# A transformer block with modulation on one core: four piece sums of the second modulation, moved from VectorE to TensorE

## What is computed

```
mod = silu(c) @ wmod                      # six rows of 1024
ga, gb = sign * max(|.|, 0.25)            # the two gates
h = layernorm(x) * (1 + ca) + sa
x = x + ga * (h @ masked(weight).T + bias)        # 1024 -> 1024
h = layernorm(x) * (1 + cb) + sb
x = x + gb * (silu(h @ gate_w.T) * (h @ up_w.T)) @ down_w.T    # 1024 -> 2752 -> 1024, int8-range weights
```

## Time and profile before

| | us |
|---|---|
| median of 3 runs | 1171.25 (1168.79 to 1171.27) |
| the profiled execution | 1171.43 |
| its span, first to last instruction | 1169.6 |
| TensorE busy | 1122.1 |
| VectorE busy | 652.5 |
| ScalarE busy | 398.3 |
| GpSimd busy | 340.8 |

### The profile page before, as it was taken

One profiled execution on the slowest core, in us unless ns is written; L12 is line 12 of the kernel. 1 busy time (PEld: TensorE's weight loads), 2 busy tenths in 40 slices (PEclk: granted clock), 3 DMA queues, 4 the chain that ended last, 5 costly groups with the idle time before them and its releaser, 6 DMA issues.

```text
span 1169.6 us, 13023 instructions
## 1 busy us (share of the span) xinstructions
PE 1122.1 (96%) x4773; PEld 529.4 (45%) x4773; DVE 652.5 (56%) x833; ACT 398.3 (34%) x718; POOL 340.8 (29%) x348
## 2 busy tenths in 40 slices
PE   5799999999988989999999999999999999999998
PEld 2544544545443434444444444444444444444444
DVE  3989957866655677767666666654442222222222
ACT  0322036655454434544544554443330000000000
POOL 1133327447634253434354344431110000000000
PEclk9799899999999999999999999999999999999999
DMA  9993221435344345755565555421644433434320
GB/s 345 401 343 79 73 71 37 108 97 164 135 157 122 99 124 168 186 138 148 131 151 139 147 151 142 107 67 42 255 147 169 151 120 139 149 115 149 106 103 36
DMA packets 88736, 167.10 MB, mean 143 GB/s; under 512 B 18592, under 2 KB 53152, under 8 KB 85984
## 3 DMA queue, kind: packets, MB, share of 16 engines
q1 hardware_dynamic: 77168, 125.88, 34.5%
q0 software_dynamic: 11504, 40.38, 11.5%
HBM read 117.47 MB, written 48.76 MB: 142 GB/s over the span
## 4 chain that ended last, share of the span: by engine, by line
PE 77%; DVE 10%; DMA 4%; issue 3%; POOL 2%; SPq 2%; ACT 1%; DVEq 1%; POOLq 0%; ACTq 0%
PE pA L1082 26%; PE pA L1178 12%; PE pB L1082 12%; PE pB L1178 12%; PE pA L962 11%; DVE work L1295 3%; DMA work<-in_L_wmod 2%; PE pB L951 2%; DMA work<-in_L_ffn_up_w 1%; DVE work L1456 1%; DVE work L1309 1%; SPq L451 1%; DVE work L1293 1%; DVE work L1393 1%; DVE small L1196 1%
## 5 line engine op out<-in xcount | busy, mean ns | idle before, releaser
L1082 PE MATMUL pA<-work 128*128 128x512 f16 x1680 | 380.7, 381 | 12.4 <-ACT work L863 6.3
L1082 PEld LDWEIGHTS pA<-work 128*128 128x128 f16 x1680 | 164.6, 98 | 214.8 <-issue 9.3
L962 PE MATMUL pA<-work 128*128 128x512 f32 x512 | 227.2, 599 | 3.1 <-ACT work L770 2.0
L1082 PE MATMUL pB<-work 128*128 128x512 f16 x752 | 176.2, 379 | 1.7 <-DVE work L1456 1.7
L962 PEld LDWEIGHTS pA<-work 128*128 128x128 f32 x512 | 96.3, 192 | 117.0 <-issue 112.3
L692 POOL DMA_DIRECT2D h_scratch<-work x84 | 64.3, 766 | 287.0 <-DVE work L1470 286.8
L1178 PE MATMUL pA<-work 128*128 128x512 f16 x672 | 147.7, 379 | 0.0
L863 ACT ACTIVATE work<-pA 128x512 f32<-128x512 f32 x126 | 75.1, 596 | 195.2 <-PE pA L1082 195.0
L1178 PE MATMUL pB<-work 128*128 128x512 f16 x630 | 138.4, 379 | 0.0
L1470 DVE SCALAR_TENSOR_TENSOR work<-work 128x512 f16<-128x512 f16 x84 | 69.5, 828 | 107.0 <-ACT work L869 107.0
L746 ACT ACTIVATE work<-pB,small 128x128 f32<-128x128 f32 x256 | 92.6, 477 | 87.4 <-PE pB L951 80.9
(11 more groups left out here) (130 smaller groups left out, 972.2 us busy)
## 6 DMA issues: line engine op xcount, KB each, us to landing
work<-h_scratch SPq DMA_DIRECT2D x16, 1376.0 KB, 6.1
h_scratch<-work POOLq DMA_DIRECT2D x84, 256.0 KB, 3.3
work<-in_L_wmod SPq DMA_DIRECT2D x10, 2048.0 KB, 17.7
work<-in_L_ffn_gate_w SPq DMA_DIRECT2D x84, 128.0 KB, 3.7
work<-in_L_ffn_up_w SPq DMA_DIRECT2D x84, 128.0 KB, 3.7
work<-in_L_ffn_down_w SPq DMA_DIRECT2D x96, 112.0 KB, 2.6
work<-in_L_attn_data SPq DMA_DIRECT2D x16, 512.0 KB, 4.4
x_scratch<-work POOLq DMA_DIRECT2D x16, 512.0 KB, 5.6
```

The costliest lines, as they stand in the source:

```text
L962: last = pe.matmul(pA[:, 2 * par(t) + h, :], hT1[par(t)][:, c, :], wT[:, c, h * H:(h + 1) * H], start=(c == 0), stop=(c == KT - 1))
L1082: last = pe.matmul(ps, w[:, m, c], bc[b][:, mv_, s, c], start=begin, stop=(i == n - 1 and c == KT // 2 - 1 and s == 1), skip_group_check=True)
```

## The change

The four pieces 6 to 9 (v = 3 and 4) are summed by `row_sum` on TensorE. The list `ROWS` numbers the row sums: 0 and 1 are the pieces 0 and 2 as before, 2 to 5 are the pieces 6 to 9. The four new sums alternate between the two banks `pB[2]` and `pB[3]`. In tile 2 TensorE makes two of them after `transpose(0, 3)`, ahead of `attend(2, 1)`, and two behind it; ahead of the first stands the wait for `ga_ready`, which was in tile 3. ScalarE copies each row, in two instructions of 256 columns, behind `turn_out(3)`; sums 4 and 5 wait until the bank is copied, and `transpose(1, 0)` in tile 3 waits until all are. `columns(3)` and `columns(4)` wait for the copies and take 1/128 as their right operand. VectorE's four `sum_half` are gone. SP waits in tile 8 for the row sums.

```
@@ -225,7 +225,7 @@
         boundT, boundp = pA[:, 3, P:2 * P], pA[:, 3, 3 * P:3 * P + 4]
         sump = [pB[:, 3, 4 * NB * g:4 * NB * (g + 1)] for g in range(2)]
 
-        rowsum = [pA[:, 0, :], pA[:, 2, :]]
+        rowsum = [pA[:, 0, :], pA[:, 2, :]] + [pB[:, 2 + k % 2, :] for k in range(4)]
         turned = [pA[:, 1, :], pA[:, 3, :], pA[:, 0, :], pA[:, 2, :]]
 
         def turned_at(u):
@@ -325,7 +325,8 @@
 
 
 
-        SUMMED = [1, 3, 4, 5, 6, 7, 8, 9]
+        SUMMED = [1, 3, 4, 5]
+        ROWS = [0, 2, 6, 7, 8, 9]
 
         TURNS = [0, 2, 1, 3, 4, 6, 5, 7]
 
@@ -404,9 +405,7 @@
             return tb_late if r in (2, 3) else tb
 
         def wait_summed(eng, m):
-
-            n = SUMMED.index(m) + 1
-            eng.wait_ge(dve_summed, n + sum(1 for k in SUMMED[:n] if 6 <= k < 10))
+            eng.wait_ge(dve_summed, SUMMED.index(m) + 1)
 
         def mask_rows(eng, r):
             w = wst[r].rearrange("p (b i) -> p b i", i=Q)
@@ -497,7 +496,7 @@
                     sp.wait_ge(xg_ready, t + 2)
                     load_x(t + 3)
                 if t == 8:
-                    wait_summed(sp, 8)
+                    sp.wait_ge(row_summed, 6)
                 if 8 <= t < 8 + EARLY:
                     load_unit(t - 8)
 
@@ -733,9 +732,23 @@
             act.wait_ge(c_loaded, 16)
             act.activation(csil, cvec, ACT.Silu).then_inc(silu_c_done, 1)
 
-            for v in range(2):
-                act.wait_ge(row_summed, v + 1)
-                act.activation(acc[v][:, 0:H], rowsum[v], ACT.Copy).then_inc(row_copied, 1)
+            def copy_row(k):
+                v, h = ROWS[k] // 2, ROWS[k] % 2
+                act.wait_ge(row_summed, k + 1)
+                if v < 2:
+                    act.activation(acc[v][:, H * h:H * (h + 1)], rowsum[k], ACT.Copy).then_inc(row_copied, 1)
+                    return
+
+                if v == 4:
+                    act.wait_ge(acc_used, 3)
+                by_tile = acc[v].rearrange("p (c a i) -> p a c i", c=KT, a=A)
+                for a in range(2):
+                    last = act.activation(by_tile[:, 2 * h + a],
+                                          rowsum[k][:, a * KA:(a + 1) * KA].rearrange("p (c i) -> p c i", c=KT), ACT.Copy)
+                last.then_inc(row_copied, 1)
+
+            copy_row(0)
+            copy_row(1)
             act.wait_ge(acc_used, 2)
             act.activation(colm[:, 0:KT], colp[:, 0:KT], ACT.Copy).then_inc(cols1_ready, 1)
             act.activation(colm[:, KT:2 * KT], colp[:, KT:2 * KT], ACT.Copy, bias=1.0).then_inc(cols1_ready, 1)
@@ -833,6 +846,9 @@
                     hi_part(t - 3)
                 if t <= LAST - 1:
                     turn_out(t + 1)
+                if t == 2:
+                    for k in range(2, 6):
+                        copy_row(k)
                 if t == 13:
                     hi_part(t - 3)
                 if t == 5:
@@ -965,15 +981,14 @@
                     last.then_inc(attn_done, 1)
 
             def columns(v, dst):
+
                 if v < 2:
-
                     pe.wait_ge(row_copied, v + 1)
                     wait_summed(pe, 2 * v + 1)
                 else:
-                    for h in range(2):
-                        wait_summed(pe, 2 * v + h)
+                    pe.wait_ge(row_copied, 2 * v - 2)
                 for c in range(KT):
-                    rhs = share if v < 2 and c < KT // 2 else one
+                    rhs = share if v > 2 or c < KT // 2 else one
                     last = pe.matmul(dst[:, c:c + 1], acc[v][:, P * c:P * (c + 1)], rhs, start=True, stop=True)
                 last.then_inc(acc_used, 1)
 
@@ -995,12 +1010,14 @@
                 pe.matmul(sump[g], blk1, msum[:, 4 * NB * g:4 * NB * (g + 1)], start=True, stop=True)\
                   .then_inc(mask_total, 1)
 
-            def row_sum(v):
-
-                pe.wait_ge(piece_loaded[2 * v], 16)
-                w = mp[2 * v].rearrange("p (t n) -> p t n", t=KT)
+            def row_sum(k):
+
+                pe.wait_ge(piece_loaded[ROWS[k]], 16)
+                if k >= 4:
+                    pe.wait_ge(row_copied, k - 1)
+                w = mp[ROWS[k]].rearrange("p (t n) -> p t n", t=KT)
                 for t in range(KT):
-                    last = pe.matmul(rowsum[v], csil[:, t:t + 1].to_broadcast([P, P]), w[:, t],
+                    last = pe.matmul(rowsum[k], csil[:, t:t + 1].to_broadcast([P, P]), w[:, t],
                                      start=(t == 0), stop=(t == KT - 1))
                 last.then_inc(row_summed, 1)
 
@@ -1057,8 +1074,12 @@
                     attend(t, 0)
                 if t <= LAST - 1:
                     transpose(0, t + 1)
+                if t == 2:
+                    pe.wait_ge(ga_ready, 1)
+                    row_sum(2)
+                    row_sum(3)
                 if t == 3:
-                    pe.wait_ge(ga_ready, 1)
+                    pe.wait_ge(row_copied, 6)
                 if t in MID:
                     transpose(1, MID[t])
                 if t == 5:
@@ -1069,6 +1090,9 @@
                     pe.wait_ge(pair_free, 2)
                     for v in (3, 4):
                         columns(v, colp2[:, KT * (v - 3):KT * (v - 2)])
+                if t == 2:
+                    row_sum(4)
+                    row_sum(5)
                 if t in END:
                     transpose(1, END[t])
 
@@ -1404,23 +1428,19 @@
             gate_a()
             normalise(0, 3)
             residual_of_evacuated(0)
-            sum_half(3, 0)
             normalise(1, 0)
             residual_of_evacuated(1)
             stats1(4)
             dve.wait_ge(scales_loaded, 16 * 2 * (A + 1))
             bound_of(2, sgs)
             bound_of(3, sus)
-            sum_half(3, 1)
             normalise(0, 4)
             residual(2)
             stats1(5)
-            sum_half(4, 0)
             normalise(0, 5)
             normalise(1, 1)
             residual(3)
             stats1(6)
-            sum_half(4, 1)
             normalise(0, 6)
             residual(4)
             cols2()
```

## The result

The changed kernel takes 1192.26 us (median of 4, 1190.75 to 1193.08) against 1170.53 (median of 4): a ratio of 1.0184, 95% interval 1.017 to 1.0197, so 21.7 us slower, where 18.6 was forecast and 1190.0 us predicted. Run again beside other kernels it was 1193.14 (median of 4) against 1170.52, 1.0199 (1.018 to 1.0218), so 22.6 us slower.

The account below looks back on a forecast made before the run. TensorE, busy 1122.1 of 1169.6 us, was taken as full: 27.5 us of sums less 8.9 us regained gives 18.6 us, so 1171.43 becomes 1190.0 us. Forecast A spans 1188 to 1191.5; C extends it down to 1186, D up to 1193.

Parts of the forecast that it names:

- TensorE pays in full: Tile 2: nothing lies idle there, so the four row sums cost their full length on TensorE, 27.5 us.
- What comes back: Tiles 2 to 5: TensorE regains only what it waited or ran slowly for, 1.85 + 2.68 + 1.70 + 2.68 = 8.9 us.
- The fourth part: First six records of attend(5, 0), slowed by the half clock, return to full speed: 2.68 us regained.
- rival D: Tile 5: the clock still falls at the one-column matmuls, without standing still; 1192.7 to 1194.4 us, chance 19%.
- the forecast A: Whole kernel: the main forecast, 1188 to 1191.5 us with 1190.0 predicted; chance 67%.
- What is late next: Tile 5: the bounds arrive with about 0.9 us left, no new wait; the 1.05 us wait for L1363 stays.
- The covers: ScalarE's copies, taken as 0.9 us a row, and the moved ga_ready wait and pieces stay hidden: cost 0.
- Later waits: From attend(5, 1) on: the same 16.8 us of TensorE waits remain, not shortened by a later start.
- Rival C: Start of gate and up products: the 3.30 and 3.69 us waits partly go; 1179.4 to 1187 us, chance 8%.
- B: 85 to 140 us: VectorE sets the pace and the sums fit in free; 1162.5 us, chance 3%.

Follow-up runs that it names:

- the first repeat: The changed kernel run again unaltered, beside other kernels on one chip: 1193.14 us; its clock was kept in tile 5.
- a5_double_columns: The changed kernel with each of the two column groups of tile 4 made twice, back to back: 1199.47 us (one run).
- b1_late_columns: The kernel before with columns(4) moved between the third and fourth matmul of attend(5, 0), the bounds' transpose behind it: 1167.22 us, ratio 0.997.
- a4_double_sums: The changed kernel with each of the four new row sums made twice, 32 more matmuls: 1219.82 us (one run).
- the eighth: The changed kernel with each of the four new row sums taking 1 of its 8 slices: 1167.05 us, ratio 0.9968 to the kernel before.
- b2_late_early_bound: The kernel before with columns(4) and bounds moved into and behind attend(5, 0), and VectorE's bounds copy ahead of normalise(0, 7): 1163.55 us, ratio 0.994.
- m1_one_sum: The kernel before with only piece 9 summed on TensorE, at the end of tile 2: 1171.43 us, ratio 1.0014.
- c_after_again: A repeat of the changed kernel, unaltered; the two repeats measured 1193.14 us and 1194.73 us.

## Why the prediction was right, and where it was off

*TensorE pays in full.* Right, and the term that decided. 27.5 us forecast, 27.47 in the trace, linear over three doses. The reading behind it was the average busy share first, then the timeline, which showed 4.53 us of waits against 28.7 us of VectorE work to be moved.

*What comes back.* Forecast 8.9 us, measured 7.35 us in the first trace. The two waits and the columns came as said (2.01, 2.68, 1.67 for 1.85, 2.68, 1.70). The fourth part, 2.68 for the six records, was mis-sized: 0.99 came in that trace, all of it in the first repeat. That is rival D, which I had at 19%. With the fall it should have been 1192.7 to 1194.4; the medians, which mix executions with and without it, are 1192.3 and 1193.1, above the 1188 to 1191.5 of the forecast A, and the fall costs 1.7 us and not 2.7 to 4.4. I had counted the fall as needing the standing still; the columns alone were enough in most executions. In the kernel before I had also told the order wrongly: the clock fell during the wait (granted at 1.00 over 138 to 139 us, 0.63 over the next, 0.50 from 140 on), ahead of the second column group and not behind it.
The Trainium skill (TensorE: Matmul & The Clock Gate, Part 1) calls the throttled clock the default that activity releases. In the doubled columns TensorE was busy by its records for 8.47 us, and the clock was granted at 0.70 and then 0.50 all the same, so a TensorE that is busy by its records was not enough here.

*What is late next.* Right in the changed kernel: the bounds were in at 167.32 and TensorE came for them at 169.85 (in the repeat that kept its clock at 168.42 and 169.26, so 0.84 us to spare, where 0.9 was forecast), and the 1.05 us wait stayed. It was wrong where I used the same reasoning in an experiment (b1_late_columns), because there I looked at VectorE's own work and not at GpSimd's, which it waits for.

*The covers.* ScalarE's two copies take 0.66 us a row, not 0.9, and stay off the path as forecast:

```profile
132.12 0.66 ACT L746 ACTIVATE work<-pB 128x256 f32<-128x256 f32 x2 [6.21 <-PE pB L1020]
139.86 2.91 ACT L759 ACTIVATE work<-pB,small 128x128 f32<-128x128 f32 x8 [7.08 <-PE pB L967]
```

The last ends at 132.78, and `turn_out(4)` waits a further 7.08 us for its transpose, as forecast. No piece and no `ga_ready` was waited for. VectorE lost 26.6 us, not 28.7: one normalisation more than before falls beside a GpSimd addition and takes 2.82 us (most take 0.81), off the path.

*Later waits.* Forecast unchanged; 16.7 us against 16.8. Rival C is refuted by these rows, in which the waits of 3.3 and 3.7 us stand as before, and by the doubled sums, B by the eighth.
The Trainium skill (Perfetto Trace Analysis, the note at its head) has it that matmul busy time is a bad measure and that the share of weight loads is to be read. That share is 45% in both kernels, which would leave TensorE half free, and yet it had no room for a single added matmul. In this kernel the start-to-start distance of the matmuls decided, and the share of weight loads would have misled.

*What the sum left out.* Some 1.7 us outside the stretch: 0.7 ahead of it and 1.0 behind. The 0.7 ahead are the landing of the second piece of `wmod`: in all thirteen traces `attend(1, 1)` starts 58.0 us (57.96 to 58.05) behind the second row sum, which waits for that piece; it starts at 24.26 before and at 24.94 after. Over all traces it starts at 23.29 to 25.70 where the program is made from the kernel before, and at 23.18 to 26.97 where it is made from the changed one, so no effect of the change can be seen in it. The part behind is one more fall of the clock, at a wait that is as long in both kernels:

```profile
424.35 1.90 PE L1082 MATMUL pA<-work 128*128 128x512 f16 x8 [2.39 <-DVE work L1456]
```

```profile
445.24 3.55 PE L1106 MATMUL pA<-work 128*128 128x512 f16 x8 [2.42 <-DVE work L1476]
```

Eight records in 1.90 and in 3.55 us, behind 2.39 and 2.42 us of waiting. The fall costs 1.7 us in all and takes the place of a wait of 0.71 us that the kernel before has at 431 us, which leaves 1.0. Over the thirteen traces the part behind `attend(5, 1)` goes roughly with these eight records, whatever stands in tiles 2 to 5: where they took 1.90 us (the kernel before, b2_late_early_bound, a4_double_sums) it was 1013.3 us, with 2.31 and 2.44 it was 1013.5 and 1013.7, and with 2.75 to 3.56 it was 1014.1 to 1015.2; the two left, m1_one_sum and b1_late_columns, had 3.10 and 2.97, and 1015.6 and 1016.1, the latter with its own fall in tile 5 counted in. So the one trace of the kernel before kept its clock in a place where ten of thirteen lost it, and with doubled sums it was kept too. I don't hold the two parts for an effect of the change.

The medians leave something open all the same. The changed kernel is 21.7 and 22.6 us slower in them, while its stretch is only 18.2 (no fall) to 19.9 us longer. With one eighth of the matmuls and with divided columns, medians and stretch agree within 0.3 us (3.9 for 4.2 us faster, 17.8 for 17.7 us slower). Scatter of the start and of the later falls can make 2 us, but no run shows that it is that.

## What to carry to other kernels

Before moving work to the fullest engine, add up from its timeline what it waits for the work now: that sum, not the busy time freed elsewhere, is all that can come back. Here it was 4.5 us of waiting (and up to 4.4 of slow clock) for 27.5 us of matmuls. The larger of the two waits and the slow clock could be had for nothing: take the late result a few matmuls later and put dense work between the light groups, and then look for what is late next, also on the engines that the late engine itself waits for. Here that gave 0.6% where the move cost 1.8%.

## What the runs showed of the hardware

One-column f32 matmuls, 0.11 us apart at the full clock, kept TensorE busy by its records, and yet the granted clock fell to 0.50 in the midst of them. In a5_double_columns they go from 164.04 to 172.51 us; the granted clock was 1.00 up to 169 us, 0.78 over the next microsecond and 0.50 from 170 us on.

How early `attend(1, 1)` starts differs by up to 3.8 us between traces whose programs do the same up to there: 81.19 and 81.30 in two, 85.00 in a5_double_columns. In the changed kernel's three executions it was 82.98, 84.08 and 83.78. What differs is when the second piece lands, for which TensorE waits at the second row sum. In the repeat c_after_again (beside the earlier trace rows, where that sum starts at 24.26 and takes 7.13 us):

```profile
26.12 10.10 PE L1020 MATMUL pA<-work,small 128*128 128x512 f32 x16 [3.14 <-DMA work<-in_L_wmod]
36.05 4.18 PE L992 MATMUL pB<-small,work 128*128 128x1 f32 x32
```

The sum starts 1.9 us later here and runs 3.0 us longer at the lower clock. Only the first counts: `attend(1, 1)` follows the start of this sum by 58.0 us in all thirteen traces, whether the sum took 7.13, 8.83 or 10.10 us. The 3.8 us of scatter are more than what this kernel's medians can tell apart. The one-column matmuls behind it stand without a wait too, and they lost the clock as well: it was 0.87 over 36 to 40 us and 0.50 over 40 to 44.
